# Local attention inside a merged block: another order of the work within a step on four engines, and the value projection one tile later

## The reference, cut to what matters

```python
h = shift_token(x)
q, k, v = jnp.split(h @ wqkv, 3, axis=-1)      # 8 heads of 64
q = l2norm(q) * qs;  k = l2norm(k) * ksc
q, k = rotary_xpos(q, k)
o = local_attention(q, k, v)                   # windows of 64 rows: own window and the one before
x = x + o @ wo
```

## Time and profile before

| | |
|---|---|
| median of 3 runs | 1297.33 us (1294.86 to 1297.55) |
| the profiled execution | 1294.97 us |
| its span, first to last instruction | 1293.2 us |
| PE busy | 1132.8 us (88%) |
| DVE, ACT, POOL busy | 893.7 us (69%), 807.7 us (62%), 672.0 us (52%) |
| mean granted clock of PE | 0.954 of full speed |

### The profile page before, as it was taken

How to read it: one execution, slowest core, us unless ns; L and a number is a source line. 1 busy time by engine, 2 the same in 40 slices (tenths; PEclk the granted TensorE clock), 3 DMA queues, 4 the chain that set the end, 5 groups by cost and what they waited for, 6 DMA issues and landing times. The chain is left out here.

```text
span 1293.2 us, 32165 instructions
## 1 busy us (share of the span) xinstructions
PE 1132.8 (88%) x10342; PEld 783.9 (61%) x10351; DVE 893.7 (69%) x3081; ACT 807.7 (62%) x2665; POOL 672.0 (52%) x1073
## 2 busy tenths in 40 slices
PE   5799994899999988798999999979679999599997
PEld 3566761566666665564666666656449999344443
DVE  4799995788888875647888888756461011589998
ACT  3688873788888884237888888843280000377776
POOL 1679885788888872107888888821252000211112
PEclk9799996999999999899999999989988999699999
DMA  6000000112221122211211111100008884100000
GB/s 217 2 3 10 10 2 12 38 42 66 50 51 45 43 49 71 64 33 44 50 44 43 43 43 43 43 13 1 8 21 313 288 273 156 34 11 12 14 12 17
DMA packets 67381, 75.51 MB, mean 58 GB/s; under 512 B 42117, under 2 KB 53313, under 8 KB 62849
## 3 DMA queue, kind: packets, MB, share of 16 engines
q1 hardware_dynamic: 67233, 73.62, 20.1%
HBM read 46.18 MB, written 2.38 MB: 38 GB/s over the span
## 5 line engine op out<-in xcount | busy, mean ns | idle before, releaser
L1167 PE MATMUL psum<-wa_wqkv,wa_hT 128*128 128x512 f32 x384 | 200.6, 607 | 0.5 <-DVE wa_tmp L1032 0.4
L1123 ACT ACTIVATE wa_p<-psum,wa_nb 128x128 f32<-128x128 f32 x512 | 180.2, 372 | 7.2 <-DVE wa_nb L1047 7.2
L1014 POOL TENSOR_TENSOR wa_p<-wa_p,wa_rrs 128x512 f32<-128x512 f32 x128 | 133.1, 1040 | 73.6 <-DVE wa_rrs L1056 73.6
L1047 DVE CUSTOM_DVE_ANT_0 psum<-psum,wa_bias 128x128 f32<-128x128 f32 x512 | 130.6, 328 | 44.3 <-PE psum L1196 44.3
L2025 PE MATMUL psum<-ex_wT,ex_hT 128*128 128x512 f32 x256 | 133.0, 602 | 0.9 <-DVE ex_yw L1964 0.3
L2050 ACT ACTIVATE ex_yw<-psum,ex_w 128x128 f32<-128x128 f32 x384 | 102.7, 397 | 41.7 <-DVE ex_total L1981 34.1
L1707 PE MATMUL psum<-cv_v,cv_toep 128*128 128x128 f32 x1024 | 118.8, 279 | 6.3 <-DMA cv_toep<-cv_zpad 6.3
L1707 PEld LDWEIGHTS psum<-cv_v,cv_toep 128*128 128x128 f32 x1024 | 117.9, 196 | 6.5 <-issue 6.5
L1123 ACT ACTIVATION_READ_ACCUMULATOR wa_p<-psum,wa_nb 128x1 f32 x512 | 109.1, 213 | 0.0
L1176 PE MATMUL psum<-ident,wa_p 128*128 128x128 f32 x512 | 83.7, 287 | 28.0 <-POOL wa_p L1014 22.5
L1176 PEld LDWEIGHTS psum<-ident,wa_p 128*128 128x128 f32 x512 | 54.5, 142 | 87.3 <-POOL wa_p L1014 66.9
(11 more groups left out here) (253 smaller groups left out, 3180.1 us busy)
## 6 DMA issues: line engine op xcount, KB each, us to landing
cv_toep<-cv_zpad SPq DMA_DIRECT2D x32, 1024.0 KB, 6.5
wa_vm<-wa_v SPq DMA_DIRECT2D x127, 128.0 KB, 2.3
wa_tabs<-in_rotations_dram SPq DMA_DIRECT2D x2, 2048.0 KB, 8.0
wa_rows<-y_rows SPq DMA_DIRECT2D x31, 128.0 KB
wa_rows<-y_rows SPq DMA_DIRECT2D x31, 127.0 KB
x_rows<-in_L_attn_x_dram SPq DMA_DIRECT2D x4, 512.0 KB, 5.9
out_dram<-x_rows SPq DMA_DIRECT2D x32, 64.0 KB, 1.5
wa_wqkv<-in_L_ffn_wqkv_dram SPq DMA_DIRECT2D x2, 768.0 KB, 11.0
```

Of the source, the lines that this page charges most:

```text
L1014: nc.gpsimd.tensor_tensor(p, p, cols_bc(rrs[:, t % 2, r, :], P), ALU.mult)\
L1047: m = nc.vector.tensor_tensor_reduce(out=s, in0=s, in1=edges, scale=-1.0, scalar=MAX_FLOAT, op0=ALU.add, op1=ALU.min, accum_out=nb[:, t % ...
L1123: e = nc.scalar.activation(pr[:, t % 2, r, h, :], sim_bank[r][:, P * h:P * h + P], ACT.Exp, bias=nb[:, t % 2, r, h:h + 1], scale=-1.0, acc ...
L1167: nc.tensor.matmul(bank, hT[:, t % 3, :], wqkv[:, INNER * k:INNER * k + INNER], start=True, stop=True).then_inc(done.sem, 1)
```

## The change

Only the order of the lists changes, with two lags and one wait:

- POOL: `scale_p(1)` now stands ahead of `add_k`.
- DVE: `o_columns` moves from the end of the step to behind `row_max(0)`, one tile later (lag 5, was 4); `reciprocal(0)` stands ahead of `rotate_q`; `rotate_k` moves behind `norms` and `reciprocal(1)`; `residual` is last. `norms`, which reads both squares and had `rotate_k` ahead of it, gets a wait of its own for `square_k`.
- ACT: `inverse_norms` is first; `square_q` and `square_k` stand together behind `exps(0)`; `values` moves to behind `k_columns`.
- PE: `scores` is first; `project_q` and `project_k` stand together behind `turn_p[1]`; `output` moves behind `turn_q`; `project_v` is one tile later (lag 2, was 1) and ahead of `turn_k`; the product `values` comes behind `turn_k`.

No instruction is added or removed, no shape and no buffer changes.

```diff
-            return Phase([(scale_q, 2), (scale_k, 2), (scale_p(0), 3), (add_q, 1), (add_k, 1), (clip, 1),
-                          (scale_p(1), 3)], first, TILES, begin=None if l else lambda: at_start(gp))
+            return Phase([(scale_q, 2), (scale_k, 2), (scale_p(0), 3), (add_q, 1), (clip, 1),
+                          (scale_p(1), 3), (add_k, 1)], first, TILES, begin=None if l else lambda: at_start(gp))
...
             def norms(t):
+                a_sk.wait(dve, t)
                 g_ss.wait(dve, t - 3)
...
-            return Phase([(row_max(0), 3), (row_max(1), 3), (rotate_q, 1), (residual, 5), (reciprocal(0), 3),
-                      (rotate_k, 1), (norms, 1), (reciprocal(1), 3), (o_columns, 4)], first, TILES,
+            return Phase([(row_max(0), 3), (o_columns, 5), (row_max(1), 3), (reciprocal(0), 3),
+                          (rotate_q, 1), (norms, 1), (reciprocal(1), 3), (rotate_k, 1), (residual, 5)], first, TILES,
...
-            return Phase([(h_columns, 0), (values, 2), (square_q, 1), (inverse_norms, 2), (p_columns(1), 4),
-                      (exps(0), 3), (q_columns, 2), (square_k, 1), (k_columns, 2), (exps(1), 3),
-                      (p_columns(0), 3)], first, TILES,
+            return Phase([(inverse_norms, 2), (h_columns, 0), (p_columns(1), 4), (exps(0), 3),
+                          (square_q, 1), (square_k, 1), (q_columns, 2), (exps(1), 3), (k_columns, 2),
+                          (values, 2), (p_columns(0), 3)], first, TILES,
...
-            return Phase([(turn_h, 0), (project_q, 1), (scores, 3), (turn_p[1], 4), (output, 5), (project_k, 1),
-                      (turn_q, 2), (values, 4), (turn_k, 2), (project_v, 1), (turn_p[0], 3)], first, TILES,
+            return Phase([(scores, 3), (turn_h, 0), (turn_p[1], 4), (project_q, 1), (project_k, 1),
+                          (turn_q, 2), (output, 5), (project_v, 2), (turn_k, 2), (values, 4),
+                          (turn_p[0], 3)], first, TILES,
```

## The result

The changed kernel takes 1275.12 us (median of 4 runs, 1272.94 to 1278.50) against 1296.09 us before (1293.41 to 1297.55; the 1297.33 given above was the median of the first three of these four runs): a ratio of 0.9843, 95% interval 0.9814 to 0.9872, so faster by 1.3 to 1.9%. The forecast was 1274, its range 1264 to 1287. The profiled execution took 1275.81 us, its span 1274.0 us, 19.2 less than before. The four runs of the changed kernel are in the order of their mean granted clocks: 1272.94 us at 0.956, 1274.43 at 0.953, 1275.81 at 0.952, 1278.50 at 0.946.

A forecast was written before the change was run, and what follows sets the result against it. A two-step loop through POOL's scale_p(1) was taken as the bound, PE's own work close below. Steps 19.3, running in 3.6 and running out 0 gave 22.9 us off 1294.97: 1272.1, as a median 1274, range 1267 to 1283.

The forecast's parts named there:

- the loop over two steps by `scale_p(1)`: Kernel before: scores to scale_p(1) to turn_p[1] and on to scores, 16.36 us for two steps, 8.18 a step.
- The step: Attention's steady state: 7.83 us instead of 8.18, over 28 steps and two layers 19.3 us gained.
- The loop on ACT: From turn_p[1] over exponentials, squares and k_columns to turn_p[0] 6.13 us, back through scores and turn_h 7.83.
- PE's own work: PE's work in one attention step, without its waits: 7.77 to 7.80 us.
- What was costed at nothing: Waits predicted free: scale_p(1) with 0.74 us spare, residual 0.39, norms on square_k, and wa_vm loads there by about 17.5.
- Running in: First turn_k to first scores in each layer: 2.2 us gained, 1.8 kept, 3.6 in all; bounds 0 and 2.5 a layer.
- Running out: Attention's end into the feed-forward part: 0 taken, bounds a loss of 4.5 us and a gain of 2 a layer.
- Rival 1: PE's turn_h waits for DVE's late residual; at 1.0 us late steps take 8.44 us, 1308 us; chance 0.07.
- Rival 2: Joints between PE groups cost more, or ACT's loop is longer: 8.05 us a step, 1287 us; chance 0.20.
- rival 3: Nothing gained: steps of 8.05 us and running out at its upper bound, 1296 us; chance 0.05.
- Rival 4: PE's joints at scores vanish, the loop falls to 7.57 us a step, 1260 us; chance 0.05.

The follow-up runs named there:

- experiment 1: Kernel before with only POOL's list changed, scale_p(1) ahead of add_k: 1284.83 us, ratio 0.9919, a step 7.978 us.
- experiment 4: Changed kernel with ACT's copy `values` moved ahead of the squares, one tile later (lag 3): 1304.84 us, a step 8.373 us.
- experiment 7: Changed kernel with q_columns on DVE, between reciprocal(0) and rotate_q, instead of on ACT: 1268.29 us, ratio 0.9776, a step 7.747 us.
- experiment 5: Changed kernel with six more 128x128 copies ahead of each residual on DVE: 1323.64 us, steps 8.547 and 8.533 us.
- experiment 3: Kernel before with POOL's and DVE's new lists and the added wait of norms, ACT's and PE's lists old: 1572.32 us, ratio 1.2121.
- experiment 6: Changed kernel with the attention's last step ahead of the feed-forward part's step 1 in DVE's stream: 1267.31 us, ratio 0.9782.
- experiment 8: Changed kernel with the second layer's tables and weights ahead of the last staging of feed-forward rows on SP's queue: 1272.38 us, ratio 0.9823.

## Why the prediction was right

**What bound the kernel.** Shown by experiment 1: the loop over two steps by `scale_p(1)`. The uneven wait of the earlier trace rows went with POOL's swap alone. That swap left a loop of one step at 7.98. Which of the other lists takes that one away was not tried apart: ACT's new order is argued by the sum given there.

**The step, 7.83 forecast, 7.876 measured.** The loop on ACT is the one named. By the rows after: 0.64 to the copy, 0.49 to the exponentials, 1.37, 0.47 and 0.48 for the squares, 0.48, 1.36, 0.83 to `turn_p[0]` make 6.12 (6.13 forecast); 0.56 and 1.03 lead on through `scores` to `turn_h` as forecast; but `turn_h` to `turn_p[1]` is 0.17 and not 0.11. That is the missing 0.05, 2.6 us over 56 steps. `turn_h` had never stood directly behind `scores`, and I took its price from a group in which it followed transposes. Experiments 4 and 7 show the loop from both sides: 0.48 more on ACT costs 0.50 a step, 0.5 less gives 0.13 and then PE is full. PE's own work, forecast as 7.77 to 7.80, is 7.747.

**What was costed at nothing.** `scale_p(1)` has 0.82 to spare (0.74 forecast); `residual` 0.48 (0.39), which experiment 5 confirms by overdrawing it; in the steps shown no engine waits for `norms` or for `wa_vm`. (The prediction has `wa_vm` there by about 17.5; its own terms, 7.6, 6.53 and 2.3, give 16.4.) Together the steps gave 16.8 us, where the prediction had 19.3.

**Running in, 3.6 forecast, 4.8 measured.** From `turn_k` to the first `scores` it is now 1.36 us (576.78 to 578.14) instead of 3.99; forecast was 1.43. The steps up to the third `scores` gain 2.4 of these 2.6 us in each layer; I had held back 0.4 of 2.2 for the first full step, and it gave back 0.2.

**Running out, 0 forecast, 4.3 and 3.1 us lost.** This is the term that was wrong, almost at its bound of 4.5 a layer. I argued that the feed-forward part's step 1 could start some 3 us earlier, "the end of PE's order there being the same". In the first layer it takes 23.79 us instead of 22.40 from the 31st `scores` to the last `output`, `output` at the lower clock costs 0.87 more and the up products 2.09 more. The granted clock was not in the sum at all. It was 0.80 and 0.85 in the two running outs, against 0.89 before. At 1.00 experiment 4 has 30.12 us with the same DVE list and the same wait, within 0.3 of the kernel before, so the loss against the kernel before came with the clock and not with the order alone; in experiment 7 the clock makes 3.37 us within one kernel. Two things stay open. What the kernel before would take there at 1.00 no run shows. And what brings the lower clock is not shown: idle stretches of 3.10 and 3.11 us in the same place left it at 1.00. The loss in the sum is thus in part an accident of the profiled execution.

**The wait for the tables**, not foreseen: 6.6 us shorter. Of these 4.9 are the gap on PE itself (8.15 us before, from the transposes at 519.95 to 528.10; 3.25 after, 516.73 to 519.98). The other 1.7 are the clock again: the group of products right behind the wait takes 4.65 us before, behind 7.55 us of idle time, at a mean granted clock of 0.59, and 2.92 after, behind 2.65, at 1.00. The two errors, 7.5 lost and 6.6 gained, nearly cancel. Part of that is no luck: the 4.3 lost in the first layer never reached the time, since the way from there on hangs on the last `residual`. The rest, 2.3 gained there (1.7 by the clock) against 3.1 lost in the second layer, is. The total was right in part for that reason: the forecast's -22.9 compares with -16.8 - 4.8 + 7.5 - 6.6 = -20.7 in the part that the change touches.

**The range.** The prediction says that 1267 to 1283 follows from the bounds of all its terms. That holds for the lower end. With steps of 7.92, nothing for the running in and 4.5 lost a layer in the running out, the upper end is 1292. The measured 1275 lies within either.

**The rivals.** Rival 1 needs 0.48 us of delay and did not come; experiment 5 shows its mechanism with its price, and experiment 3 a steeper form of it. Rival 2 fell: the joints add 0.05, not 0.2. Of rival 3 the running out came, the slow steps didn't. Rival 4 fell: nothing vanished at `scores`. `turn_p[0]` to `scores` takes 0.56 us, and a group of four transposes ahead of a projection or an `output` 0.44 (407.06 to 407.50, 409.21 to 409.65), so a joint of 0.12 stays in every step, also where PE never idles (experiment 7). The rule of the Trainium skill, the page "TensorE: Matmul & The Clock Gate", section "Step-by-step: what each phase is for", that weight loads are pulled ahead of running products where the row groups don't conflict or the load goes to the background buffer, would have hidden it; at this joint between full and half arrays the trace doesn't show that. Whether the joint is a weight load is not shown either.

## What to carry to other kernels

With an order written by hand on several engines, follow each loop through all of them and over as many steps as it spans: steps that alternate in length point to a loop over two. A list is good only together with the others: the same DVE list took part in a gain of 1.6% and, beside PE's old list, in a loss of 21%. And check the ends of a loop as carefully as its steady state: a wait there costs its own length, it can be followed by a stretch at half the clock in one place and not in another like it, and it can hide behind, or uncover, a load that is issued a fixed time after another event. So read the granted clock of a stretch before you put a difference down to the order.

## What the runs showed of the hardware

- In the changed kernel an idle stretch of PE of 2.82 us, in a part where it was sparsely busy before, was followed by products at half the rate: pairs of 128x512 products start 1.71 us apart (494.50, 496.21) instead of 0.86, from 492.64 to about 498.5 us. The granted clock is 0.50 there, that is 1.2 instead of 2.4 GHz, and 0.83 as the mean of the window. With 0.21 us of idle time in the same place it was 1.00.
- The length of the idle stretch did not decide it. In the same place 3.10 us (experiment 4) and 3.11 us (experiment 7, first layer) left the clock at 1.00. In the feed-forward part the group behind 7.55 us of idle time ran at a mean of 0.59, the one behind 5.13 us (experiment 6) at 0.61, and the one behind 2.65 us at 1.00.
- The price: one order of work takes 28.98 us at 1.00 and 32.35 us at a mean of 0.84 (experiment 7), and the runs of the changed kernel differ by 5.6 us, from a mean clock of 0.956 to one of 0.946.
- A `turn_h` (one 128x128 transpose) adds 0.17 us behind `scores` and 0.11 behind other transposes: joints between full and half arrays show on both sides.
- The row copy of L875 holds SP's queue for 6.55 us, and in experiment 8, issued while the tables were loading, for 11.64 us.
